# Attention block, one core: scores as six 64-row products, steps of two slots

## The reference

```python
h = group_norm(x, 32 groups) * norm_scale + norm_bias   # statistics over tokens and 16 channels
q, k, v = split(h @ qkv_w + qkv_b, 3)                   # each 1024 x 512
q, k, v = (z.reshape(16 * 8, 1024, 64) for z in (q, k, v))   # a plain reshape
w = softmax((q * s) @ (k * s).T)                        # s * s = 1/8
out = x + (w @ v).reshape(16, 1024, 512) @ proj_w + proj_b
```

## Time and profile before

| | |
|---|---|
| three executions | 3835.63, 3845.33, 3846.1 us; median 3845.33 |
| the profiled execution, its own time | 3851.28 us |
| its span, first to last instruction | 3848.4 us |
| mean granted TensorE clock | 0.994 of full |
| busy | PE 3663.7 us, DVE 2780.5, ACT 2435.3, POOL 1829.1 |
| 1024 slots | 3.76 us of span each |
| DMA queue of SP | 254224 packets, 638 MB, 69.7% of 16 engines |

### The profile page before, as it was taken

How to read it: one execution, slowest core, us unless ns; L and a number is a source line. 1 busy time by engine, 2 the same in 40 slices (tenths; PEclk the granted TensorE clock), 3 DMA queues, 4 the chain that set the end, 5 groups by cost and what they waited for, 6 DMA issues and landing times.

```text
span 3848.4 us, 77013 instructions
## 1 busy us (share of the span) xinstructions
PE 3663.7 (95%) x24128; PEld 2805.1 (73%) x24128; DVE 2780.5 (72%) x3473; ACT 2435.3 (63%) x4753; POOL 1829.1 (48%) x3018
## 2 busy tenths in 40 slices
PE   6999999999999999999999999999999999999998
PEld 5777777777777777777777777777777777777775
DVE  4777777777777777777777777776776777777776
ACT  6666666566665766666666666566665666665763
POOL 4455454444454544445445445444454544454551
PEclk9999999999999999999999999999999999999999
DMA  3767677777676767777777676766767677677766
GB/s 116 183 164 179 166 173 170 167 178 168 165 173 166 181 161 173 168 170 180 166 168 167 167 184 158 172 166 166 180 163 172 164 169 181 158 178 168 170 161 166
DMA packets 255911, 648.82 MB, mean 169 GB/s; under 512 B 73872, under 2 KB 73872, under 8 KB 255376
## 3 DMA queue, kind: packets, MB, share of 16 engines
q1 hardware_dynamic: 254224, 638.35, 69.7%
q10 hardware_dynamic: 1152, 4.19, 0.3%
HBM read 71.84 MB, written 33.55 MB: 27 GB/s over the span
## 4 chain that ended last, share of the span: by engine, by line
PE 84%; SPq 4%; ACT 4%; issue 3%; DVE 2%; DMA 1%; POOL 0%; ACTq 0%; POOLq 0%; DVEq 0%
PE pv_ps L412 23%; PE s_ps L379 13%; PE s_ps L381 11%; PE c_ps L452 5%; PE c_ps L453 5%; PE c_ps L454 5%; SPq L343 4%; PE pv_ps L392 4%; ACT staged L526 3%; PE c_ps L437 3%; PE c_ps L435 3%; PE c_ps L436 3%; PE c_ps L463 2%; PE c_ps L465 2%; PE c_ps L464 2%
## 5 line engine op out<-in xcount | busy, mean ns | idle before, releaser
L638 DVE TENSOR_REDUCE neg_max<-s_ps 128x1 f32<-128x1024 f32 x1024 | 1242.2, 1213 | 940.8 <-PE s_ps L381 940.4
L512 ACT ACTIVATE probs<-s_ps,neg_max 128x1024 f32<-128x1024 f32 x1024 | 1143.8, 1117 | 1217.3 <-DVE neg_max L638 1206.2
L619 DVE STREAM_TRANSPOSE turned<-probs 128x1024 f32<-128x1024 f32 x1024 | 1263.8, 1234 | 3.3 <-DMA probs_t<-turned 2.5
L412 PE MATMUL pv_ps<-probs_t,v 128*64 128x256 f32 x8192 | 994.1, 385 | 10.0 <-DMA probs_t<-turned 10.0
L526 ACT ACTIVATE staged<-c_ps,qk_bias 64x256 f32<-64x256 f32 x2048 | 956.8, 467 | 30.9 <-PE c_ps L454 10.1
L761 POOL CAST attn_hi<-attn 128x256 fp32r<-128x256 f32 x256 | 102.0, 398 | 1448.7 <-DVE attn L632 1200.4
L412 PEld LDWEIGHTS pv_ps<-probs_t,v 128*64 128x64 f32 x8192 | 562.4, 138 | 308.3 <-issue 81.0
L452 PE MATMUL c_ps<-h_hi,w_hi 128*128 128x256 f32 x2048 | 582.6, 284 | 64.1 <-ACT staged L526 57.7
L453 PE MATMUL c_ps<-h_lo,w_hi 128*128 128x256 f32 x2048 | 578.0, 282 | 0.0
L454 PE MATMUL c_ps<-h_hi,w_lo 128*128 128x256 f32 x2048 | 577.2, 282 | 0.0
L452 PEld LDWEIGHTS c_ps<-h_hi,w_hi 128*128 128x128 f32 x2048 | 388.1, 189 | 100.8 <-ACT staged L526 74.5
(11 more groups left out here) (75 smaller groups left out, 5790.4 us busy)
## 6 DMA issues: line engine op xcount, KB each, us to landing
probs_t<-turned SPq DMA_DIRECT2D x4096, 128.0 KB, 2.3
x_res<-in_x SPq DMA_DIRECT2D x128, 256.0 KB, 2.7
result<-x_res SPq DMA_DIRECT2D x128, 256.0 KB, 2.6
x_next<-in_x SPq DMA_DIRECT2D x120, 256.0 KB, 2.8
probs_t<-in_L_conv_qkv_w ACTq DMA_DIRECT2D x4, 768.0 KB, 8.7
turned<-in_x SPq DMA_DIRECT2D x4, 512.0 KB, 12.8
probs_t<-in_L_conv_proj_w ACTq DMA_DIRECT2D x4, 256.0 KB, 13.8
v_bias<-in_L_conv_qkv_b SPq DMA_DIRECT2D x1, 256.0 KB, 16.9
```

What stands on the lines that cost most here:

```text
L412: last = nc.tensor.matmul(pv_ps[side][CH * par:CH * (par + 1), 0, :], v_sb[:, ring_of(i, parity), CH * chunk:CH * (chunk + 1)], p_t[:, par ...
L512: nc.scalar.activation(probs[k % 2][:, :], s_ps[k % 2][:, :], ACT.Exp, bias=neg_max[:, k % 4:k % 4 + 1], accum_out=row_sum[:, (k // HALF) ...
L619: nc.vector.transpose(dst, probs[(k - 1) % 2][:, :].rearrange("p (k b j) -> p k b j", k=CHUNKS, b=QUADS)).then_inc(probs_turned, 1)
L638: nc.vector.tensor_reduce(neg_max[:, k % 4:k % 4 + 1], s_ps[k % 2][:, :], AX.X, ALU.max, negate=True).then_inc(max_ready, 1)
```

## The change

- **Steps.** ScalarE and VectorE work in steps of two slots, run at even k. ScalarE: inverse copy, both exps, norm, then staging and x copies of both slots. VectorE: both maxima, scaling, v of the slot before, first transpose, v or projection, second transpose, inverse, statistics. TensorE makes the scores of both slots at the even one, then large(k), small(k), large(k+1), small(k+1) with spread and attend as before.
- **Scores** are three products, q_hi k_hi, q_hi k_lo, q_lo k_hi, of 64 rows, each for both halves of the partitions: six of 64-row 128x512. q is kept on both halves in q_hi and q_lo; k only once, even chunks on rows 0-63 and odd ones on 64-127. The term lo x lo is gone.
- **k is staged once**: one activation of 128x256, one cast and one subtraction on GpSimd.
- **Inverses** are widened by VectorE to 128x256 (a reciprocal of a broadcast operand) and turned by two TensorE transposes; row_sum has four places instead of two; the inverse is taken six slots after the half began.
- **Residual**: one buffer; loaded at 7 and 15 (mod 16), bias added at 9 and 1, stored at 4 and 12.
- Statistics at other slots, moves one slot earlier, x tiles loaded two slots after the last use, norm at slot 0 of a pair.

```diff
-STAT_SLOTS = [1, 10, 14, 17, 21, 26, 36, 38]
-AGGREGATE_SLOT = 40
-GROUP_MEAN_SLOT = 41
-GROUP_VAR_SLOT = 43
-AFFINE_SLOT = 44
+STAT_SLOTS = [1, 5, 9, 13, 21, 29, 37, 41]
+AGGREGATE_SLOT = 42
+GROUP_MEAN_SLOT = 44
+GROUP_VAR_SLOT = 46
+AFFINE_SLOT = 47
-MOVE_LAG = 5
+MOVE_LAG = 4
+INVERT_LAG = 6
...
             def slot(b, k):
-                if k % HALF == MOVE_LAG % HALF:
-                    move_half(b, k)
-                if k % 16 == 0:
-                    load_residual(b, 2 * (k // 16) - 1)
-                if k % 16 == 8:
-                    load_residual(b, 2 * (k // 16))
+                if k == 0:
+                    load_x_tile(b, 0)
                 if k % 16 == 4:
                     store(b, 2 * (k // 16) - 2)
                 if k % 16 == 12:
                     store(b, 2 * (k // 16) - 1)
-                if k == 0:
-                    load_x_tile(b, 0)
-                if k in STAT_SLOTS[:-1]:
-                    load_x_tile(b, STAT_SLOTS.index(k) + 1)
+                if k % HALF == MOVE_LAG % HALF:
+                    move_half(b, k)
+                if k % 16 == 7:
+                    load_residual(b, 2 * (k // 16) - 1)
+                if k % 16 == 15:
+                    load_residual(b, 2 * (k // 16))
+                if k - 2 in STAT_SLOTS[:-1]:
+                    load_x_tile(b, STAT_SLOTS.index(k - 2) + 1)
...
-                q = q_st[c % 2][:, at, c // 2, :]
-                for par in range(2):
-                    dst = s_ps[k % 2][:, par * C:(par + 1) * C]
-                    nc.tensor.matmul(dst, q, k_hi[par][:, at, :, :].rearrange("p j t -> p (j t)"),
-                                     start=True, stop=False)
-                    last = nc.tensor.matmul(dst, q, k_lo[par][:, at, :, :].rearrange("p j t -> p (j t)"),
-                                            start=False, stop=True)
+
+                for n, (q, keys) in enumerate(((q_hi, k_hi), (q_hi, k_lo), (q_lo, k_hi))):
+                    for par, rows in enumerate((slice(0, CH), slice(CH, P))):
+                        last = nc.tensor.matmul(s_ps[k % 2][:, par * C:(par + 1) * C], q[c % 2][rows, at, c // 2, :],
+                                                keys[rows, at, :, :].rearrange("p j t -> p (j t)"),
+                                                start=(n == 0), stop=(n == 2))
...
-                for i in range(HALF):
-                    par, u = i % 2, i // 2
-                    last = nc.tensor.matmul(pv_ps[side][CH * par:CH * (par + 1), 1, u * P:(u + 1) * P],
-                                            inv_sum[:, side, i:i + 1].broadcast_to([P, CH]), ident[:, :],
-                                            start=True, stop=True)
+                for u in range(2):
+                    last = nc.tensor.transpose(pv_ps[side][:, 1, u * P:(u + 1) * P], inv_wide[:, u * P:(u + 1) * P],
+                                               ident[:, :])
...
-                if within(s, N_SLOTS):
+                if k % 2 == 0 and within(s, N_SLOTS):
                     scores(b, k)
+                    scores(b, k + 1)
...
+                if n >= KT:
+                    nc.scalar.activation(staged[n % 2][:, 0, :], c[:, 0:2 * P], ACT.Identity,
+                                         bias=qk_bias[:, n:n + 1]).then_inc(qk_staged, 1)
+                    return
...
-                at_least(dve, inv_full, half - 1)
-                nc.vector.reciprocal(inv_sum[:, n % 2, :], row_sum[:, n % 2, :]).then_inc(inv_ready, 1)
+                at_least(dve, inv_full, half)
+                sums = row_sum[:, n % 4, :].rearrange("p (s a) -> p s a", a=1).broadcast_to([P, HALF, CH])
+                nc.vector.reciprocal(inv_wide[:, :].rearrange("p (s c) -> p s c", s=HALF), sums).then_inc(inv_ready, 1)
...
-            def slot(b, k):
+            def step(b, k):
                 s = SPB * b + k
                 if within(s, N_SLOTS):
-                    dve.wait_ge(scores_full, s + 1)
...
+                    largest(b, k)
+                    largest(b, k + 1)
                 if k % HALF == EVAC_LAG % HALF and within(s - EVAC_LAG, N_SLOTS):
                     scale_attn(b, k)
...
+                if k % 16 == 0:
+                    if k > 0:
+                        take_v(b, k - 1)
+                    elif not before_start(b):
+                        take_v(b - 1, SPB - 1)
+                if within(s, N_SLOTS):
+                    turn(b, k)
+                kind, _, part = large_unit(k + 1)
+                if kind == "v" and large_unit(k + 1)[1] == 1:
+                    take_v(b, k + 1)
+                if kind == "proj":
+                    take_proj(b, k + 1)
+                if within(s, N_SLOTS):
+                    turn(b, k + 1)
+                if k % HALF == INVERT_LAG % HALF and within(s - INVERT_LAG, N_SLOTS):
                     invert(b, k)
```

More of the change, by code:

```diff
@@ L176, in attention_block @@
         pool_chain = sem("pool_chain")
-        x_loaded = [sem(f"x_loaded{i}") for i in range(XRING)]
-        stored = [sem(f"stored{i}") for i in range(XRING)]
+        x_loaded = sem("x_loaded")
+        stored = sem("stored")
         x_start_loaded = [sem(f"x_start_loaded{i}") for i in range(PPB)]
@@ L288, in batches, with in_steps @@
                 slot(BATCHES, k)
+        def in_steps(step):
+            return lambda b, k: step(b, k) if k % 2 == 0 else None
         def at_least_aside(engine, sem, count):
@@ L587, in _ @@
                 act.dma_start(pw_stage[t], proj_w[t * P:(t + 1) * P, :]).then_inc(pw_loaded, 16)
-            batches(act, slot)
+            batches(act, in_steps(step))
         @block.vector
@@ L635, in slot, with take_proj, step @@
+            def take_proj(b, k):
+                n, h = large_unit(k)[1], proj_block(b, k)
+                if not within(h, N_BLOCKS):
+                    return
+                dve.wait_ge(proj_full, h + 1)
+                dve.wait_ge(residual_ready, h + 1)
+                nc.vector.tensor_tensor(x_res[:, :], bank(k, LARGE)[:, :], x_res[:, :], ALU.add).then_inc(out_ready, 1)
+            def step(b, k):
                 s = SPB * b + k
                 if within(s, N_SLOTS):
-                    dve.wait_ge(scores_full, s + 1)
@@ L657, in slot @@
-                if kind == "proj" and part == 1:
-                    h = proj_block(b, k)
-                    if within(h, N_BLOCKS):
-                        dve.wait_ge(proj_full, h + 1)
-                        dve.wait_ge(residual_ready, h + 1)
-                        r = x_res[:, n % XRING, :]
-                        nc.vector.tensor_tensor(r, bank(k, LARGE)[:, :], r, ALU.add).then_inc(out_ready, 1)
+                if k % 16 == 0:
[3 more added lines that the diff above has]
+                        take_v(b - 1, SPB - 1)
@@ L698, in statistics @@
                                                    ALU.add, ALU.add).then_inc(group_taken, 1)
-            batches(dve, slot)
+            batches(dve, in_steps(step))
         @block.gpsimd
@@ L732, in split_qk, with src @@
                 done = 2 * KT * g + n
-                tiles = q_st if n < KT else k_hi
-                def src(par, rows=slice(0, P)):
-                    return staged[n % 2][rows, par, :].rearrange("p (i t) -> p i t", i=2)
+                def src(par):
+                    return staged[n % 2][:, par, :].rearrange("p (i t) -> p i t", i=2)
                 at_least_aside(pool, qk_staged, done + 1)
-                for par in range(2):
-                    last = nc.gpsimd.tensor_copy(tiles[par][:, both, j, :], src(par))
+                if n < KT:
+                    for par in range(2):
+                        last = nc.gpsimd.tensor_copy(q_hi[par][:, both, j, :], src(par))
+                else:
+                    last = nc.gpsimd.tensor_copy(k_hi[:, both, j, :], src(0))
                 last.then_inc(qk_rounded, 1)
@@ L799, in slot @@
                     affine(b)
-                if m == 15:
-                    add_bias(b, 2 * pair)
+                if m == 9:
+                    add_bias(b, 2 * pair - 1)
+                if m == 1:
+                    add_bias(b, 2 * pair - 2)
             batches(pool, slot)
```

127 lines of the change are left out of this document (59 added, 68 removed).

## The result

| | kernel before | changed kernel |
|---|---|---|
| median of four executions | 3842.02 us | 4022.09 us (4016.13 to 4022.77) |
| profiled execution, its span | 3851.28, 3848.4 us | 4022.31, 4020.6 us |
| mean granted TensorE clock | 0.994 | 0.959 |

The ratio is 1.0467 (95% interval 1.0447 to 1.0487): 4.7% slower. The forecast was 3742 us, with a range of 3600 to 3870. It was wrong, in sign too.

A forecast was written before the change was run, and what follows sets the result against it. TensorE was taken as the bound, busy 3663.7 of 3848.4 us. The terms -241 - 67 + 90 - 106 + 221 = -103 gave 3748 us for the profiled execution, 3742 for the median, range 3600 to 3870.

The forecast's parts named there:

- (a): Scores: six 64-row products run as pairs on opposite row halves, three pitches of 0.235 us per slot: -241 us.
- (b): Inverses before attend: two transposes, attend starting 0.43 us after the last product: -67 us.
- (c): TensorE mode changes: one more per step of two slots, 512 times 0.175 us: +90 us.
- (d): TensorE waits that go: x tiles -27, old shared-bank waits -68, idle counted from modelled ends 11 more: -106 us.
- (f): Priced at nothing: wide reciprocal at 0.39 us, k staged once, earlier moves and one residual buffer, all fitting into slack.
- Rival three: Wide reciprocal on VectorE is slow: some 120 us per 1.0 us above 0.39, 3935 us at 2.0; chance 0.10.
- (e): New TensorE waits for shared banks, staged by ScalarE only after both exps or emptied late by VectorE: +221 us.
- Rival one: The new TensorE waits on shared banks are hidden; at half of them 3632 us; chance 0.15.
- Rival two: Row halves in the scores take turns, six pitches instead of three: about 4390 us; chance 0.20 together with the slow reciprocal.
- wrong if VectorE's maxima come without idle time before them: Sign against the forecast: VectorE's maxima were to be still waiting for scores, its slack covering the extra work.

The follow-up runs named there:

- e1_narrow: Changed kernel with the reciprocal taken of 128x4 sums and a copy widening it to 128x256: 3874.35 us, ratio 1.0074 to the kernel before.
- e7_pad: Changed kernel with 144 already fulfilled waits (72 instructions) added ahead of TensorE's loop, moving only the loop's code: 3943.89 us, ratio 1.0252 to the kernel before.
- e11_stage: Kernel with five edits together (e8_all), ScalarE staging the first unit between the two exps in five steps: 3569.23 us, ratio 0.9271 to the kernel before.
- e9_full: Kernel with five edits together (e8_all), its scores as four products of 128 rows: 3758.65 us, ratio 0.9769 to the kernel before.
- e10_perslot: Kernel with five edits together (e8_all), scores made slot by slot instead of two by two: 3984.49 us, ratio 1.0352 to the kernel before.
- e8_all: Changed kernel with narrow reciprocal, moved statistics, v ahead of maxima, later group means and moved loop code: 3663.82 us, ratio 0.9525 to the kernel before.
- e4_warm: Changed kernel with TensorE computing the qk units at slots 5, 21 and 37 twice: 3922.37 us, ratio 1.0201 to the kernel before.

## Why the prediction was wrong

Against the 3748 us forecast for the profiled execution, 4022 is 274 more. By the split: clock 142, which no term of the sum held; waits 57 (332, where 149.5 - 27 - 68 + 221 = 275 was forecast); stops at the loop 39, not held either; dense work 38 (-191, where (a), (b), (c) and the 11 of (d) make -229). Taken out alone, the slow reciprocal is worth 148 us (e1_narrow) and the loop's second stop 78 (e7_pad).

- **(f), the wide reciprocal at 0.39 us: failed.** It was priced by a product of the same size; it took 1.71 us. Rival three had the mechanism. Its rate, 120 us per us of reciprocal, times 1.28, is 154, and e1_narrow gives 148. That these are so close is in part luck: the rate counted waits alone, and they are 96 of the 148; 45 are clock, which it left out. Its 0.10 was too little: that four elements tell little, and an upper bound of 10.1 us, stood in the text.
- **The clock: not in the sum, the largest term.** Every wait was priced at its own length. In this kernel the three long ones of a batch (3.07 to 3.42 us idle, and the loop's second stop) bring a stretch at the 1.2 GHz level each in nearly every batch, those of 2.38 us in 8 of 30 cases, those of 2.69 in one of 16. (e) itself gave 3.1 us for unit 45, and the kernel before already had a wait of 3.1, with 6.8 us at 0.50 behind it; I did not read the granted clock there. With the narrow reciprocal 97 us of clock loss are left over the kernel before's (120 - 23): of its loss, 53 are at the loop, 27 behind unit 45, 22 behind the waits for v at slot 48 and 14 behind those at statistics products.
- **The loop's stop: not in the sum.** The kernel before shows it, 13 times, and I read it as a fixed cost. The changed code got a second one; with its clock it costs 78 us (e7_pad, which pays 6 for its own added instructions). Nothing in the diff tells that; an allowance for the stop, from nothing to a doubling, belonged in the range.
- **(e), waits on banks: place and mechanism right, sizes right with the narrow reciprocal** (193 against 221), and 282 with the wide one. For the wide one the text put 0.35 us for a late VectorE into the wait at slot 5 alone. Rival one, that they are hidden, did not come; e11_stage shows what it takes.
- **(a) and (c), row halves: right.** -132 by e9_full, where the sum had -151; the changes of mode are 0.21 instead of 0.175, the pitch 0.23 instead of 0.235. These 19 us are half of the 38 that the dense work is short; the other half is not placed. Rival two, taking turns, fell with the first pair. Steps of two carry it (e10_perslot). The Trainium skill, "TensorEngine Tiling (Array Packing)", section "Key Properties", says that different tiles work independently and that a change of mode drains the engine. The trace agrees with both, with 0.23 us for a pair and 0.20 to 0.21 more for a change.
- **(b), inverses: right** in TensorE's work, 0.43 from the last product to attend.
- **(d), waits that go: right** for x; the old bank waits went into the new ones.
- The transfers of (f), 16 moves a slot earlier and the one residual buffer, cost nothing that shows: 4.9 and 1.5 us of waits on moves in the changed kernel, 8.0 in e8_all.

Of the signs listed, "wrong if VectorE's maxima come without idle time before them" was the one that struck: in the steps behind a reciprocal they do (2056.95 above), in most others not (723.7 us of waiting for scores, in the groups above).

## What to carry to other kernels

Price an operation by rows of that operation, and widen after an expensive one, not before it: a narrow reciprocal and a copy took 0.43 us where the wide one took 1.71. A wait on TensorE costs its length and can bring a stretch of half clock besides, so look in the trace at the clock behind the longest waits before adding some. Here the loss to the clock was 165 us with waits of 2.4 to 3.4 us in every batch (changed kernel), and 18 when those on staging were at most 1.3 us and the second stop was gone (e11_stage). The same wait can have such a stretch behind it in one kernel and none in the next, so removing one wait tells little about the clock by itself. When a large change is slower than its parts, split the span into waits, stops, clock and rest: here the rest was 191 us better all along, and five small edits turned 4.7% slower than before into 4.7% faster, and with the early staging and the loop written out it is 8.4%.

## What the runs showed of the hardware that I had not expected

- The change of batch in a loop stops TensorE for 2.0 to 2.3 us in the rows shown (1.8 to 3.0 over the 13 of the kernel before), and in some kernels a second time, 3.6 us from one start to the next (2034.79 to 2038.40). 72 idle instructions ahead of the loop removed the second stop and took 6.4 us once themselves; writing the loop out removed both.
- Waits of TensorE of 3.07 and 3.42 us in the changed kernel came with the 1.2 GHz level, for 6.7 us in the windows shown, in 29 of 29 cases. Waits of 2.69 us at slot 48 did in 1 of 16 there, in 14 of 16 in e4_warm; of 3.07 us in 6 of 14 in e7_pad; of 1.55 us in 5 of 15 in e8_all.
- A reciprocal of 128x256 took 1710 ns, of 128x4 135 ns; a copy that widens 128x4 to 128x256 took 294 (e1_narrow).
- e4_warm: TensorE doing 69 us of useless products ended 22 us earlier than e7_pad, which is otherwise nearest to it.
